# Three handoffs of a graph-network kernel reordered, its closing checks moved inside, and graph 1 prepared early

## What is computed

```
h = relu(layernorm(x));  x = x + L0(h, adj)    # averaging over neighbours twice, two batch norms
h = relu(layernorm(x));  x = x + L1(h, adj)    # attention, scores leaky(s_i + t_j), values W h
h = relu(layernorm(x));  x = x + L2(h, adj)    # attention, scores leaky(h_i a h_j), values h
h = relu(layernorm(x));  x = x + L3(h, adj)    # attention like L1, then elu
```

## Time and profile before

| | us |
|---|---|
| median of 3 runs | 1579.3 (1578.58 to 1580.75) |
| the profiled execution, its own time | 1582.55 |
| its span, first to last instruction | 1580.8 |
| TensorE busy | 1409.4 (89%) |
| VectorE busy | 1140.9 (72%) |
| ScalarE busy | 828.4 (52%) |
| GpSimd busy | 386.2 (24%) |
| mean granted TensorE clock | 0.952 of full |

### The profile page before, as it was taken

How to read it: one execution, slowest core, us unless ns; L and a number is a source line. 1 busy time by engine, 2 the same in 40 slices (tenths; PEclk the granted TensorE clock), 3 DMA queues, 4 the chain that set the end, 5 groups by cost and what they waited for, 6 DMA issues and landing times. The chain is left out here.

```text
span 1580.8 us, 33117 instructions
## 1 busy us (share of the span) xinstructions
PE 1409.4 (89%) x12740; PEld 1269.6 (80%) x12740; DVE 1140.9 (72%) x3276; ACT 828.4 (52%) x1825; POOL 386.2 (24%) x337
## 2 busy tenths in 40 slices
PE   5799998899846979999999999999999999999674
PEld 5799998555435869989998999899988999899574
DVE  4566664778635578888888888888888888876733
ACT  4677776122224555564655656656557465563320
POOL 6333430000000323303313133132230331312400
PEclk9999999899957989999999999999999999999786
DMA  9989991367811213223143131331322314202101
GB/s 207 228 194 209 211 208 68 134 235 252 283 35 47 81 41 81 59 78 99 35 107 86 50 94 35 101 94 41 97 67 77 89 35 107 61 21 68 41 9 34
DMA packets 109601, 161.98 MB, mean 102 GB/s; under 512 B 9472, under 2 KB 61312, under 8 KB 107392
## 3 DMA queue, kind: packets, MB, share of 16 engines
q1 hardware_dynamic: 85248, 117.86, 25.9%
q0 software_dynamic: 19584, 33.56, 11.6%
q10 hardware_dynamic: 4608, 8.39, 1.5%
HBM read 151.40 MB, written 41.94 MB: 122 GB/s over the span
## 5 line engine op out<-in xcount | busy, mean ns | idle before, releaser
L851 POOL TENSOR_TENSOR wts_B<-wts_B,off 128x1024 f32<-128x1024 f32 (+7 forms) x128 | 180.0, 1431 | 345.8 <-PE ps L1424 345.8
L1441 PE MATMUL ps<-hP_A,wts_A 128*128 128x129 f32 x2048 | 250.1, 277 | 6.1 <-DVE wts_A L922 3.3
L1441 PE MATMUL ps<-hP_C,wts_C 128*128 128x129 f32 x2048 | 244.6, 280 | 11.1 <-DVE wts_C L922 11.1
L1441 PEld LDWEIGHTS ps<-hP_C,wts_C 128*128 128x128 f32 x2048 | 238.7, 195 | 14.7 <-DVE wts_C L922 12.2
L1441 PEld LDWEIGHTS ps<-hP_A,wts_A 128*128 128x128 f32 x2048 | 239.3, 193 | 8.4 <-DVE wts_A L922 5.1
L1441 PE MATMUL ps<-hV,wts_B 128*128 128x129 f32 x2048 | 244.3, 275 | 1.6 <-ACT xC L1238 1.6
L1441 PEld LDWEIGHTS ps<-hV,wts_B 128*128 128x128 f32 x2048 | 237.1, 192 | 1.8 <-ACT xC L1238 1.8
L922 DVE SCALAR_TENSOR_TENSOR wts_C<-row_C,least_C,ring_C 128x1024 f32<-128x1024 f32 x128 | 173.1, 1366 | 2.5 <-ACT row_C L1204 1.5
L922 DVE SCALAR_TENSOR_TENSOR wts_A<-row_A,least_A,ring_A 128x1024 f32<-128x1024 f32 x128 | 160.8, 1274 | 9.3 <-ACT row_A L1204 8.2
L293 ACT ACTIVATE maskT<-ps 128x1024 fp8e4<-128x1024 bf16 x128 | 131.3, 1026 | 57.0 <-PE ps L335 46.1
L347 PE MATMUL ps<-x,adj_b 128*128 128x129 f16 x896 | 120.9, 223 | 18.1 <-ACT whn L276 14.6
(11 more groups left out here) (229 smaller groups left out, 2711.7 us busy)
## 6 DMA issues: line engine op xcount, KB each, us to landing
adj_b<-in_adj POOLq DMA_DIRECT2D x120, 256.0 KB, 9.8
maskT_scratch<-maskT SPq DMA_DIRECT2D x16, 1024.0 KB, 6.8
ring_A<-maskT_scratch SPq DMA_DIRECT2D x64, 256.0 KB, 3.1
off<-maskT_scratch SPq DMA_DIRECT2D x32, 512.0 KB, 6.5
ring_C<-maskT_scratch SPq DMA_DIRECT2D x64, 256.0 KB, 3.3
xa<-in_x SPq DMA_DIRECT2D x16, 512.0 KB, 4.6
whT_scratch<-whT_s ACTq DMA_DIRECT2D x32, 256.0 KB, 6.4
whT_b<-whT_scratch SPq DMA_DIRECT2D x16, 512.0 KB, 4.8
```

The lines of the kernel that those rows point to most:

```text
L851: pool.tensor_tensor(w, w, off_fp8[:, k, k * P:N], ALU.mult).then_inc(S["B", "up"], 1)
L1441: last = nc.tensor.matmul(Q_SLOTS[c // 2 % 2][:, c % 2, 0:PW], wts[x][:, j, c * P:c * P + P], src[:, j, :], start=(j == 0), stop=(j == T - 1))
```

## The change

It has these parts.

1. **C's maximum.** VectorE runs `columns("C")` before `leaky(1)` instead of behind it.
2. **C's row power.** ScalarE runs the first `row_power("C")` behind `keep_scores` 5 to 7 instead of ahead of them.
3. **A's maximum.** VectorE runs `columns("A")` and `exponents("A")` together, ahead of `shifts("B")`, and `shares("B", 1)` ahead of `weights("C", 5)`.
4. **Graph 1.** The norm of graph 1 is made in pass -1 and its attention prepared in pass 0 between the tiles of graph 0's A, instead of behind them. Its q is turned in pass -1 too.
5. **The new end.** Most checks move to VectorE between passes 8 and 9 (`early_limits`), the last to pass 18 (`late_limits`, `decide`). SyncE no longer waits for the stores inside the stage; the semaphores are not cleared; the three blocks of the general version become one, whose end waits for the stores.

Parts 1, 2 and 3, the three handoffs, as code:

```diff
@@ VectorE, run @@
+                        if CA:
+                            columns("C", i - 2)
                         if GW:
                             leaky(i - 1, 1)
                         if CA:
-                            columns("C", i - 2)
                             exponents("C", i - 2)
...
                         if CA:
                             weights("C", i - 2, 4)
+                        if nextA and i != 0:
+                            columns("A", i + 1)
+                            exponents("A", i + 1)
                         if AA:
                             shifts("B", i)
-                        if nextA:
-                            columns("A", i + 1)
+                        if GW:
+                            shares("B", i - 1, 1)
                         if CA:
                             weights("C", i - 2, 5)
-                        if GW:
-                            shares("B", i - 1, 1)
-                        if nextA:
-                            exponents("A", i + 1)
@@ ScalarE, run @@
                             keep_scores(i - 1, 4)
-                        if CA:
-                            row_power("C", i - 2, 0)
-                        if GW:
                             keep_scores(i - 1, 5)
                             keep_scores(i - 1, 6)
                             keep_scores(i - 1, 7)
+                        if CA:
+                            row_power("C", i - 2, 0)
```

Part 4, and the calls that it takes from their old places (there the condition `nextA` becomes `nextA and i != 0`):

```diff
@@ VectorE, run @@
+                        if i == 0:
+                            columns("A", 1)
+                            exponents("A", 1)
...
+                        if i == -1:
+                            shifts("A", 0)
+                            first_sum(1)
+                            dve.drain()
+                            stats("A", xA[1], 0)
+                            stats("A", xA[1], 1)
+                            dve.wait_ge(S["A", "h"], 1)
+                            moments("A")
+                            shifts("A", 1)
@@ ScalarE, run @@
                             scaled("A", i, 1)
+                            if i == 0:
+                                row_power("A", 1, 0)
+                                row_power("A", 1, 1)
                             scaled("A", i, 2)
...
+                        if i == -1:
+                            normed("A", 1, xA[1], 0)
+                            normed("A", 1, xA[1], 1)
...
+                        if i == -1:
+                            act.wait_ge(S["A", "wh_made"], 1)
+                            relu_hT("A", 1, "C", 0)
...
                     scale_q(0)
+                    scale_q(1)
@@ TensorE, run @@
+                        if i == -1:
+                            turn_q(0)
+                            turn_q(1)
+                        if i == 0:
+                            pe.wait_ge(S["A", "prod"], 1)
+                            turn_h("A", 1, hN, free_p, 1, "hT")
                         for c in range(T):
                             if AA:
                                 weigh("A", i, c)
-                            if c == 0 and nextA:
+                            if i == 0:
+                                if c == 0:
+                                    values("A", 1, free_p, 0, T)
+                                if c == 1:
+                                    highest("A", 1, free_p, 1)
+                                if c in (2, 3):
+                                    rows("A", 1, free_p, c - 2)
+                            if c == 0 and nextA and i > 0:
                                 turn_q(i + 1)
```

Part 5:

```diff
@@ SyncE, third stage @@
                     save(B - 1)
-                    for k in range(3):
-                        sp.wait_ge(S["C", "out"][k], len(range(k, B, 3)) * 16)
@@ VectorE @@
                         if post:
                             highest_share("C", 2)
+                        if i == B + 2:
+                            late_limits()
                         if post and not GW:
                             elu_positive()
+                        if i == B + 2:
+                            decide()
...
                         run(i)
+                        if i == B // 2:
+                            early_limits()
@@ behind the third stage @@
-        retire_sems()
...
+        with nc.allow_non_contiguous_dma("column blocks of adj"), nc.Block() as block:
+            @block.sync
+            def _(sp):
+                with sp.If(sp.value_load(redo[0:1, 0:1]) != 0):
...
+                    again1_sync(sp)
+                    next_part(sp, 1)
+                    again2_sync(sp)
+                    next_part(sp, 2)
+                    again3_sync(sp)
+                sp.end_ifs()
+                for k in range(3):
+                    sp.wait_ge(S["C", "out"][k], len(range(k, B, 3)) * 16)
```

More of the change, by code:

```diff
@@ new lines, in again1_scalar @@
+        def again1_scalar(act):
+            with act.Fori(0, B) as b:
+                with act.Fori(0, T) as t:
+                    n = b * T + t
+                    act.wait_ge(logits_ready, n + 1)
+                    nc.scalar.activation(pro[:, :], sco[:, :], ACT.Exp, bias=nmax[:, 0:1],
+                                         accum_out=rsum[:, 0:1]).then_inc(exp_ready, 1)
+                    act.wait_ge(wT_made, n + 1)
+                    nc.scalar.copy(proT[:, :, :].rearrange("p t c -> p (t c)"), pair(1)).then_inc(wT_ready, 1)
+                    act.wait_ge(whT_made, n + 1)
+                    nc.scalar.copy(whT[:, :], ps[:, 4, 0:P]).then_inc(whT_ready, 1)
@@ new lines, in again1_tensor @@
+        def again1_tensor(pe):
+            with pe.Fori(0, B) as b:
+                with pe.Fori(0, T) as t:
+                    n = b * T + t
+                    pe.wait_ge(adj_real, n + 1)
+                    for r in range(T):
+                        last = nc.tensor.transpose(pair(0)[:, r * P:r * P + P], tmp[:, r * P:r * P + P], ident[:, :])
+                    last.then_inc(adjT_made, 1)
+                    pe.wait_ge(w_ready, n + 1)
+                    for r in range(T):
+                        last = nc.tensor.transpose(pair(1)[:, r * P:r * P + P], pro[:, r * P:r * P + P], ident[:, :])
+                    last.then_inc(wT_made, 1)
+                    pe.wait_ge(wT_ready, n + 1)
+                    for r in range(T):
+                        last = nc.tensor.matmul(ps[:, 4, 0:P], hg[:, r, :], proT[:, r, :], start=(r == 0), stop=(r == T - 1))
+                    last.then_inc(whT_made, 1)
+                    pe.wait_ge(whT_ready, n + 1)
+                    for o in range(O2):
+                        last = nc.tensor.matmul(ps[:, 5, o * P:o * P + P], k1_sb[:, o * P:o * P + P], whT[:, :],
+                                                start=True, stop=True)
+                    last.then_inc(y_made, 1)
@@ new lines, in again2_scalar, with again2_tensor @@
+        def again2_scalar(act):
+            with act.Fori(0, B) as b:
+                with act.Fori(0, T) as t:
+                    n = b * T + t
+                    act.wait_ge(rk_made, n + 2)
+                    nc.scalar.copy(RK[:, bass.ds(t, 1), :].rearrange("p a d -> p (a d)"), ps[:, 0, 0:P]).then_inc(rk_ready, 1)
+        def again2_tensor(pe):
+            with pe.Fori(0, B) as b:
+                with pe.Fori(0, T) as t:
+                    n = b * T + t
+                    pe.wait_ge(yn_ready, n + 1)
+                    for o in range(O2):
+                        last = nc.tensor.matmul(ps[:, 0, 0:P], yn[:, o, :], k2_sb[:, o, :], start=(o == 0), stop=(o == O2 - 1))
+                    last.then_inc(rk_made, 1)
+                    pe.wait_ge(rk_ready, n + 1)
+                pe.wait_ge(w_in, b * 16 + 16)
+                for c in range(CH):
+                    for t in range(T):
+                        last = nc.tensor.matmul(ps[:, 2 + c, :], RK[:, t, :], w_all[:, t, c * HALF:(c + 1) * HALF],
+                                                start=(t == 0), stop=(t == T - 1))
+                last.then_inc(pT_made, 1)
```

782 lines of the change are left out of this document (364 added, 418 removed).

## The result

The changed kernel takes 1562.53 us (median of 4 runs, 1560.2 to 1564.65); the kernel before took 1578.94 us beside it (4 runs, 1577.65 to 1580.75). The ratio is 0.9895, with a 95% interval from 0.9877 to 0.9913: 16.4 us faster, where 17.7 were forecast. The sum came out near the truth. Its terms did so less, as the experiments show.

The account below looks back on a forecast made before the run. TensorE bounds the steady passes, so only its pauses can be won. The terms -12.2 - 3.9 - 5.6 + 1.4 + 1.6 + 1.0 = -17.7 us led from 1579.3 to 1561.6, range 1554 to 1572.

Parts of the forecast that it names:

- handoff of A: Passes 2 to 14: TensorE's pause before A's maximum moves to the second `rows`; 0.3 us a pass saved, 3.9 in all.
- handoffs of C: Passes 2 to 15: pauses before C's maximum and the last `gram` go; 0.4 us a pass saved, 5.6 in all.
- graph 1 early: Pass 0: steps added among graph 0's products cost 3.75 us, a shorter chain to B's transpose wins 2.3; net +1.4.
- pass 1: Pass 1: VectorE waits for TensorE in A's exponents, so sf_B slips and TensorE waits at the second `rows`; +1.6 us.
- early checks: Between passes 8 and 9: nine small VectorE instructions delay C's first share; +1.0 us, between 0 and 2.2.
- the end: End of the program: checks run beside VectorE work, one jump of 2.44 us beside the last store; -12.2 us.
- the new wait for `row_A`: Before A's second `rows`: a new TensorE wait of about 1.4 us, as a sign of the moved pause.
- The rival in which the jump costs what all three did: End of the program: the merged jump costs 7.3 us, so the end gains 8.4 instead of 12.2; 1565.4 us, chance 0.08.
- The rule at sf_B: GpSimd's power before sf_B: small VectorE steps beside it add nothing; if they added 0.96 us, A's handoff would cost +8.6.
- The pauses go altogether: Steady passes: TensorE's waits at A and C vanish, 29.7 us saved instead of 9.5; 1541 us, chance 0.10.
- The handoffs give nothing: Steady passes: the next step takes over the waits, or sf_B slips by the 0.3 won; 1571 us, chance 0.11.
- Slower: Every pass: VectorE waits in A's exponents and sf_B slips 3.2 us; +36.4 us over 13 passes, 1602 us, chance 0.03.

Follow-up runs that it names:

- e2: The kernel before with part 3 alone (A's maximum and exponents ahead of B's shifts), in every pass; 1574.22 us, ratio 0.9957.
- e4: The kernel before with parts 1 and 2 alone (C's maximum and C's row power moved); 1577.3 us, ratio 0.9977.
- e6: The changed kernel with parts 1 to 3 undone, leaving the new end and graph 1 early; 1571.56 us, ratio 0.9936.
- e5: The kernel before with part 5 alone (the new end and the early and late checks); 1570.42 us, ratio 0.9938.
- e10: The kernel before with parts 1 and 2, and C's `exps` moved behind the copy of score product 3; 1577.35 us in one run.
- e1: The changed kernel with ScalarE's first row power of A moved between the two halves of hV from pass 1 on; 1549.32 us, ratio 0.9797.

## Why the prediction was right, point by point

| term | forecast | measured |
|---|---|---|
| handoff of A | -0.3 x 13 = -3.9 | -0.47 x 13 = -6.1 (e2) |
| handoffs of C | -0.4 x 14 = -5.6 | -0.22 x 14 = -3.1 (e4) |
| graph 1 early | +1.4 | +1.25 (e6 against e5) |
| pass 1 | +1.6 | +1.33 |
| early checks | +1.0 | +0.93 (e5) |
| the end | -12.2 | -9.8 (mean of six kernels -9.4) |
| sum | -17.7 | -15.5 |

The changed kernel's profile, from the first scaling of q to the end, is 17.0 us shorter than that of before. 1.2 of them are the kernel before's own: its pass from 1344.09 us on took 65.61 us at a clock of 0.97, where the same pass took 64.39 in e5. The 15.8 that are left agree with the sum of the terms. Of the signs that the prediction named, the new wait for `row_A` (1.35 us for 1.4), the wait for `peak_A` and the shorter pass (0.67 for 0.7) came true; the last `gram` waits 0.24 us instead of under 0.1, and the last store is issued 6.6 us before the end instead of 4.

**The handoff of A** was right in its place and its kind: the pause moves to the second `rows` and is 1.54 us there, forecast 1.4. The size was half again too small. I counted the 0.23 us that `scaled("B")` waited for its share. It gained 0.32, as it began 1.88 us behind the start of hV (673.03 to 674.91) and now begins 1.56 behind it (669.35 to 670.91). And ScalarE's next step, `exps`, also waited, for te. The timeline of the kernel before has it:

```profile
675.30 0.22 DVE L900 TENSOR_SCALAR te_A<-cols_A,top 128x8 f32<-128x8 f32 x1
```

```profile
675.56 0.22 ACT L1197 ACTIVATE hP_A<-te_A 128x8 f32<-128x8 f32 x1
```

Te ended at 675.52, and `exps` began 0.65 us behind `scaled`, where it now follows by 0.50: that is 0.15 more. The two make the 0.47. From sf_B to the second `rows` it was 5.11 us and is 4.63.

**The handoffs of C** were forecast at almost twice their size. The sentence that the next product "can't begin earlier than TensorE's own queue allows" is the step that failed: it is the copy in its slot that holds it, and `exps` later on ScalarE doesn't change that (e10). The two errors, 2.2 us too little for A and 2.5 too much for C, cancel by luck; a pass is 0.67 us shorter, forecast 0.7.

**Graph 1 early** has the right net with the wrong parts, as told above: a step left out (+1.74) against products that slowed by less than was said (+2.06 for +3.75).

**The end** is the largest miss in the sum, 2.4 us. The three blocks were priced alike from their sum of 7.3 us, and the one jump at 2.44. But the third block had 4.5 of it (TensorE loads the flag at 1573.8, 1575.2 and 1576.3, the span ends at 1580.8), and its jump kept its price: from TensorE's load of the flag at 1553.0 to the end of the span it is 5.4 us, so 3.0 us stand behind the landing where I took 0.5. The rival in which the jump costs what all three did is nearer: it says 7.8 us from store to end and the forecast 4.0, where 6.9 are measured. Its reason, that a body three times as long needs more fetches, is not what the blocks show, as two of the three parts are cheap to jump over.

**The rule at sf_B**: GpSimd's power takes 2.63 us beside the small steps of VectorE, 2.60 before. At most 0.03 us were added, and the 0.96 of the rival were not. This is what the row said. The Trainium skill ("GPSIMD Engine Reference", section "Specifications") names two SBUF inputs or a two-port mode as the conditions; that `us` and `te` work in no such mode was taken for granted, and no run here shows it.

**The other rivals.** "The pauses go altogether" (1541) was wrong for this change, and e1 shows that it was one step of ScalarE away. "The handoffs give nothing" (1571) is what e6 measures without them (1571.56). "Slower" needs sf_B to slip in every pass; it came 0.03 us behind GpSimd's power.

## What to carry to other kernels

When a pause is removed, list every other wait on the way to the next product of the bound engine, also those of 0.2 us: the second one is hidden by the first, and each edit alone shows only the smaller part (0.47 and 0.21 us here, 1.67 together). Follow the chain through the engine that does the steps in between, and move its urgent step ahead of work that nobody waits for. A sum for several like blocks isn't a price for each; look at the queue's own waits and at the jump instruction's duration. And where a net agrees with its forecast, compare its parts too: in pass 0 two errors made the right number.

## What I had not expected

The jump over code that never runs costs time by what that code is: 0.2 to 0.4 us on TensorE over the first or the second part, 3.4 to 5.2 over the third or over all. The 1.1 us that SyncE waits for the store are the same whether the store landed 3.0 us before the end (changed kernel) or 4.5 (e1: issued at 1540.93, landed after 3.6, span 1549.0), because the store takes 3.6 us in both; the wait behind it, for TensorE, is 2.7 us in the one and 4.3 in the other and sets the end. And the time to reach the third stage, which no edit touches, ranges from 433.0 to 440.4 us over the profiles, and the granted clock of the first passes differs too, so whole times of single profiles say little about an edit of 1 to 3 us, while lengths of passes tell 0.03 us apart.
